# Direct maxima in the first five score units, and half of the score masks added by VectorE instead of by a product with the identity

## What is computed

```python
def _L0_xattn_ref(q, k, v, mask, Wq, bq, Wk, bk, Wv, bv, Wo, bo):
    query = _split_heads(q @ Wq.T + bq)
    key_ = _split_heads(k @ Wk.T + bk)
    value = _split_heads(v @ Wv.T + bv)
    scores = jnp.einsum('bhqd,bhkd->bhqk', query, key_) / jnp.sqrt(jnp.asarray(D_K, query.dtype))
    scores = jnp.where(mask == 0, jnp.asarray(NEG, scores.dtype), scores)
    attn = jax.nn.softmax(scores, axis=-1)
    ctx = jnp.einsum('bhqk,bhkd->bhqd', attn, value)
    return ctx.transpose(0, 2, 1, 3).reshape(...) @ Wo.T + bo

x = x + mixer(layernorm(x))
x = x + _L0_xattn_ref(layernorm(x), ctx_1024, ctx_1024, mask, ...)
x = x + experts(layernorm(x))
```

## Time and profile before

| What | Value |
|---|---|
| median of three runs | 418.87 us (418.56 to 420.62) |
| the profiled execution, its own time | 422.17 us |
| its span in the trace | 420.4 us |
| TensorE busy in the span | 356.0 us (85%) |
| VectorE busy | 262.3 us (62%) |
| ScalarE busy | 146.0 us (35%) |
| GpSimd busy | 144.6 us (34%) |
| mask products in the score stages (L1322) | 80 of 0.39 to 0.40 us each as modelled |
| fillers (L1296) | 64, 15.4 us busy |
| exponentials (L707) | 80, 0.600 us each |

### The profile page before, as it was taken

How to read it: one execution, slowest core, us unless ns; L and a number is a source line. 1 busy time by engine, 2 the same in 40 slices (tenths; PEclk the granted TensorE clock), 3 DMA queues, 4 the chain that set the end, 5 groups by cost and what they waited for, 6 DMA issues and landing times.

```text
span 420.4 us, 5562 instructions
## 1 busy us (share of the span) xinstructions
PE 356.0 (85%) x1896; PEld 235.4 (56%) x1909; DVE 262.3 (62%) x628; ACT 146.0 (35%) x276; POOL 144.6 (34%) x150
## 2 busy tenths in 40 slices
PE   1546678579987999779996899999999899999995
PEld 1333345343464535445454543687788688888883
DVE  6595376882297924971249831576779766666662
ACT  2503404816634265005531146222221323223221
POOL 7331213562012130011003020356354565666563
PEclk9985676979999999999798799999899999999998
DMA  4203650331004210153001200321100242220000
GB/s 109 68 1 81 174 192 1 94 72 38 2 0 115 54 37 0 40 122 93 0 2 50 94 16 2 125 51 50 50 27 25 68 123 69 82 64 26 27 0 25
DMA packets 22216, 23.84 MB, mean 57 GB/s; under 512 B 5117, under 2 KB 17341, under 8 KB 21973
## 3 DMA queue, kind: packets, MB, share of 16 engines
q1 hardware_dynamic: 21805, 23.29, 20.2%
q10 hardware_dynamic: 384, 0.20, 0.2%
HBM read 20.11 MB, written 3.18 MB: 55 GB/s over the span
## 4 chain that ended last, share of the span: by engine, by line
PE 60%; DVE 21%; ACT 5%; issue 4%; DMA 4%; POOL 4%; ACTq 1%; SPq 0%; POOLq 0%; DVEq 0%
DVE nmax_mask L984 6%; PE pC L1337 4%; PE pS L1322 4%; PE pC L1334 4%; PE pS L1319 3%; PE pS L268 3%; PE pS L270 3%; PE pS L269 3%; PE pG L1116 2%; PE pS L1286 2%; PE pA L268 2%; PE pS L1289 2%; PE pB L268 2%; PE pB L270 2%; PE pB L269 2%
## 5 line engine op out<-in xcount | busy, mean ns | idle before, releaser
L586 POOL TENSOR_TENSOR xi_lo<-xi_f,xi_hi 128x512 fp32r<-128x512 f32 x43 | 55.8, 1299 | 53.4 <-ACT xi_hi L739 53.2
L984 DVE TENSOR_REDUCE nmax_mask<-pS 128x3 f32<-128x462 f32 (+1 forms) x96 | 52.7, 578 | 18.1 <-PE pS L1289 17.2
L707 ACT ACTIVATE prob<-pS 128x512 f32<-128x512 f32 x80 | 42.4, 600 | 33.4 <-PE pS L1322 30.3
L739 ACT CAST xi_hi<-xi_f 128x512 fp32r<-128x512 f32 x43 | 26.7, 621 | 65.8 <-DVE xi_f L1039 65.8
L1039 DVE TENSOR_TENSOR xi_f<-sig,pS 128x512 f32<-128x512 f32 x64 | 44.0, 688 | 3.9 <-PE pS L270 0.6
L1286 PE MATMUL pS<-k_stack,q_stack 72*128 72x154 bf16 x256 | 36.7, 249 | 3.2 <-DMA q_stack<-q_scr 3.1
L586 POOL TENSOR_TENSOR act_lo<-xi_f,act_hi 128x512 fp32r<-128x512 f32 x21 | 27.5, 1310 | 27.1 <-ACT act_hi L739 27.1
L1289 PE MATMUL pS<-mbias,ident_bf 128*128 128x462 bf16 (+1 forms) x96 | 36.3, 378 | 0.0
L1286 PEld LDWEIGHTS pS<-k_stack,q_stack 72*128 72x128 bf16 x256 | 22.0, 107 | 12.1 <-issue 7.1
L1283 PE MATMUL pS<-mbiasT,ident_bf 128*128 128x128 bf16 x72 | 17.5, 243 | 11.7 <-DVE nmax_mask L984 11.4
L739 ACT CAST act_hi<-xi_f 128x512 fp32r<-128x512 f32 x21 | 13.0, 620 | 41.0 <-DVE xi_f L1039 41.0
(11 more groups left out here) (332 smaller groups left out, 846.3 us busy)
## 6 DMA issues: line engine op xcount, KB each, us to landing
prob<-w_scr SPq DMA_DIRECT2D x16, 256.0 KB, 3.3
q_stack<-q_scr SPq DMA_DIRECT2D x9, 384.0 KB
q_scr<-q_parts SPq DMA_DIRECT2D x12, 128.0 KB, 2.4
k_stack<-k_scr SPq DMA_DIRECT2D x36, 40.0 KB
res<-in_x_dram SPq DMA_DIRECT2D x4, 256.0 KB, 4.6
prob<-in_L_ffn_wg_dram SPq DMA_DIRECT2D x1, 1024.0 KB, 5.9
prob<-in_L_ffn_wp_dram SPq DMA_DIRECT2D x1, 1024.0 KB, 8.3
ctx_in<-in_L_ffn_wo_dram SPq DMA_DIRECT2D x4, 256.0 KB, 3.1
```

The source lines that it names most:

```text
L586: pool.tensor_tensor(hid_lo[u % NHID], hid[:, u % 2, :], f32(hid_hi[u % NHID]), ALU.subtract).then_inc(s_hidlo, 1)
L707: act.activation(prob[:, (NSB * b + n) % NBUF, :], score_bank(b, NSA + n)[:, :], ACT.Exp).then_inc(s_exp, 1)
L739: act.copy(hid_hi[u % NHID], hid[:, u % 2, :]).then_inc(s_hidhi, 1)
L984: dve.tensor_reduce(nmax[:, qt, hs[0]:hs[-1] + 1], score_bank(b, n)[:, 0:len(hs) * KEYS].rearrange("p (h k) -> p h k", k=KEYS), AX.X, ALU. ...
```

## The change

"keep_busy" is taken out. In its first place come the products over 72 rows and the masks of units 0 to 2 ("scores_early", EARLY = 3). The maxima of units 0 to 4 (DIRECT = 5) are not taken from rows of `q_stack` but added by one more product each, of `mT` (48 rows) with a 48 x 128 matrix of zeros and ones that sums the three parts of the right head: `head_rows` for a single head, `rest_rows` for the four. These wait for the copy to `mT` alone. Unit 5 waits for the rows of the DMA, which SP starts now instead of ScalarE, behind the query fetch of the same batch; in batch 3 the gate rows of experts 4 to 7 are moved behind them. Of the 20 units of a batch, units 3, 5, 6, 8, 10, 11, 13, 15, 16 and 18 have no mask product: VectorE adds the mask as it copies the bank to `prob`, and the exponential then reads and writes `prob`. ScalarE does that exponential one slot later than before, behind the exponential of the next unit where that one reads PSUM. `head_rows` and `rest_rows` are built by two reductions on VectorE ahead of batch 0's "max_split".

```diff
@@ -276,7 +279,29 @@
+        BY_PE, BY_DVE = range(2)
+        MASK_BY = [BY_PE] * 3 + [BY_DVE, BY_PE] + [BY_DVE, BY_DVE, BY_PE, BY_DVE, BY_PE] * (G - 1)
+        N_DVE = MASK_BY.count(BY_DVE)
...
+        DIRECT, EARLY = 5, 3
+        def exps_in(n):
+            late = [n - 1] if n > 0 and MASK_BY[n - 1] == BY_DVE else []
+            return ([] if MASK_BY[n] == BY_DVE else [n]) + late
+        EXP_ORDER = [u for n in range(NSB) for u in exps_in(n)]
+        assert sorted(EXP_ORDER) == list(range(NSB))
+        def exps_until(u):
+            return EXP_ORDER.index(u) + 1
+        def masked_until(u):
+            return MASK_BY[:u + 1].count(BY_DVE)
@@ -358,11 +383,10 @@
                 slots[u].append(("scores_max", b, u))
-            slots[NSA] += [("max_split", b, 0)]
+            slots[NSA] += [("max_split", b, 0)] + [("scores_early", b, u) for u in range(EARLY)]
...
-            slots[NSA] += [("keep_busy", b, 6)]
@@ -393,7 +417,6 @@
-            slots[B0 - 1] += [("keep_busy", b, 10)]
@@ -476,15 +499,28 @@
-                        for e in range(E):
-                            if e == 4:
-                                sp.wait_ge(s_pv, G * NB)
+                        for e in range(E // 2):
...
+                elif step == "max_rows":
+                    sp.wait_ge(s_mTc, b + 1)
+                    if b > 0:
+                        sp.wait_ge(s_mrow, 16 * PARTS * b)
+                    if b >= 2:
+                        sp.wait_ge(s_sb, NSB * (b - 1))
+                    for p_ in range(PARTS):
+                        sp.dma_start(q_stack[b % 2][MROW + p_:MROW + p_ + 1, :, :],
+                                     mT[p_ * H:(p_ + 1) * H, :]).then_inc(s_mrow, 16)
+                elif step == "weigh" and (b, n) == (NB - 1, G - 1):
+                    sp.wait_ge(s_pv, G * NB)
+                    for e in range(E // 2, E):
+                        fetch_gate(0, e)
@@ -692,20 +728,20 @@
-                    act.wait_ge(s_mTc, b + 1)
-                    for p_ in range(PARTS):
-                        act.dma_start(q_stack[b % 2][MROW + p_:MROW + p_ + 1, :, :],
-                                      mT[p_ * H:(p_ + 1) * H, :]).then_inc(s_mrow, 16)
                 elif step == "scores":
-                    act.wait_ge(s_sb, NSB * b + n + 1)
-                    before = NSB * b + n - NBUF
-                    if before >= 0:
-                        act.wait_ge(s_pv, before // 5 + 1)
-                    else:
-                        act.wait_ge(s_wsplit, EXPERT_STEPS)
-                    act.activation(prob[:, (NSB * b + n) % NBUF, :], score_bank(b, NSA + n)[:, :], ACT.Exp
-                                   ).then_inc(s_exp, 1)
+                    for u in exps_in(n):
+                        before = NSB * b + u - NBUF
+                        if MASK_BY[u] == BY_DVE:
+                            act.wait_ge(s_added, N_DVE * b + masked_until(u))
+                            src = prob[:, (NSB * b + u) % NBUF, :]
+                        else:
+                            act.wait_ge(s_sb, NSB * b + u + 1)
+                            if before >= 0:
+                                act.wait_ge(s_pv, before // 5 + 1)
+                            else:
+                                act.wait_ge(s_wsplit, EXPERT_STEPS)
+                            src = score_bank(b, NSA + u)[:, :]
+                        act.activation(prob[:, (NSB * b + u) % NBUF, :], src, ACT.Exp).then_inc(s_exp, 1)
@@ -833,6 +870,14 @@
             for step, b, n in STEPS:
+                if step == "max_split" and b == 0:
+                    dve.wait_ge(s_ident, 1)
+                    dve.tensor_reduce(head_rows[:, :],
+                                      ident[0:PARTS * H, 0:PARTS * H].rearrange("p (a h) -> p h a", a=PARTS),
+                                      AX.X, ALU.max)
+                    firsts = ident[0:PARTS * H, 0:PARTS * H].rearrange("p (a h) -> p h a", a=PARTS)[:, 0:4, :]
+                    dve.tensor_reduce(rest_rows[:, :].rearrange("p (c k) -> p c k", c=4)[:, :, 0:K1],
+                                      firsts.unsqueeze(2).broadcast_to([PARTS * H, 4, K1, PARTS]), AX.X, ALU.max)
@@ -998,6 +1043,16 @@
+                elif step == "scores" and MASK_BY[n] == BY_DVE:
+                    u = NSB * b + n
+                    dve.wait_ge(s_sb, u + 1)
+                    if u >= NBUF:
+                        dve.wait_ge(s_pv, (u - NBUF) // 5 + 1)
+                    else:
+                        dve.wait_ge(s_wsplit, EXPERT_STEPS)
+                    bias = mbiasT_rem if SB_UNITS[n][1] is None else mbiasT
+                    dve.tensor_tensor(prob[:, u % NBUF, :], score_bank(b, NSA + n)[:, :], bias[:, :], ALU.add
+                                      ).then_inc(s_added, 1)
@@ -1124,7 +1179,41 @@
                     else:
-                        pe.wait_ge(s_exp, NSB * row + k - NSA + 1)
+                        u = k - NSA
+                        if MASK_BY[u] == BY_DVE:
+                            pe.wait_ge(s_added, N_DVE * row + masked_until(u))
+                        else:
+                            pe.wait_ge(s_exp, NSB * row + exps_until(u))
+            def score_products(b, n, rows):
+                g, j = SB_UNITS[n]
+                whole = rows == DEEP
+                by_pe = MASK_BY[n] == BY_PE
+                bank_free(b, NSA + n)
+                dst = score_bank(b, NSA + n)
+                if j is None:
+                    for c in range(4):
+                        last = pe.matmul(dst[Q * c:Q * (c + 1), :], k_stack[b % 2][0:rows, 4 * g + c, K0:KPAD],
+                                         q_stack[b % 2][0:rows, 4 * g + c, :], start=True, stop=whole and not by_pe,
+                                         skip_group_check=True)
+                    bias = mbiasT_rem
+                else:
+                    last = pe.matmul(dst[:, :], k_stack[b % 2][0:rows, 4 * g + j, 0:K0],
+                                     q_stack[b % 2][0:rows, 4 * g + j, :], start=True, stop=whole and not by_pe,
+                                     skip_group_check=True)
+                    bias = mbiasT
+                if by_pe:
+                    last = pe.matmul(dst[:, :], ident_bf[:, :], bias[:, :], start=False, stop=whole,
+                                     skip_group_check=True)
+                return last
+            def less_max(b, n):
+                g, j = SB_UNITS[n]
+                assert g == 0
+                rows = rest_rows[:, :] if j is None else head_rows[:, j:j + 1].broadcast_to([PARTS * H, P])
+                return pe.matmul(score_bank(b, NSA + n)[:, :], rows, mT[:, :],
+                                 start=False, stop=True, skip_group_check=True)
@@ -1303,24 +1392,20 @@
+                elif step == "scores_early":
+                    score_products(b, n, STACK)
...
-                    g, j = SB_UNITS[n]
                     if n == 0:
+                        pe.wait_ge(s_mTc, b + 1)
+                    elif n == DIRECT:
...
-                    bank_free(b, NSA + n)
-                    dst = score_bank(b, NSA + n)
-                    if j is None:
-                        for c in range(4):
-                            pe.matmul(dst[Q * c:Q * (c + 1), :], k_stack[b % 2][:, 4 * g + c, K0:KPAD],
-                                      q_stack[b % 2][0:DEEP, 4 * g + c, :], start=True, stop=False, skip_group_check=True)
-                        bias = mbiasT_rem
-                    else:
-                        pe.matmul(dst[:, :], k_stack[b % 2][:, 4 * g + j, 0:K0], q_stack[b % 2][0:DEEP, 4 * g + j, :],
-                                  start=True, stop=False, skip_group_check=True)
-                        bias = mbiasT
-                    pe.matmul(dst[:, :], ident_bf[:, :], bias[:, :], start=False, stop=True, skip_group_check=True
-                              ).then_inc(s_sb, 1)
+                    if n >= EARLY:
+                        last = score_products(b, n, STACK if n < DIRECT else DEEP)
+                    if n < DIRECT:
+                        last = less_max(b, n)
+                    last.then_inc(s_sb, 1)
```

4 lines of the change are left out of this document (added).

## The result

The changed kernel takes **425.57 us** (median of 4 runs, 422.37 to 427.08) against 419.06 us (4 runs, 418.56 to 420.62) for the kernel before: a ratio of **1.0131**, 95% interval 1.0096 to 1.0167. The forecast was 415.2 us with a range up to 420.8. The change makes the kernel 1.3% slower. The profiled execution took 422.37 us, the shortest of the four, with a mean granted clock of 0.901; the others had 0.897, 0.889 and 0.889. The profiled execution of before (422.17 us, clock 0.926) was longer than every timed one of that kernel. So the two profiles nearly agree in length (420.6 and 420.4 us of span), and their difference must not be read as the change's.

The account below looks back on a forecast made before the run. TensorE was taken as never free in the score stages, ScalarE as second limit, VectorE late at batches 1 to 3. Batches of -2.5, +2.6, -4.0, +0.2 gave -3.7: profiled 422.17 to 418.5, hence 415.2 us, range 411.2 to 420.8.

Parts of the forecast that it names:

- The clock: TensorE's clock at batch starts without fillers: one fall, in batch 1 after a 4.1 us gap, +1.7 us; none elsewhere.
- Rival (b): Clock falls in batches 2 and 3 also, 1.5 us each, and reductions miss their slot: 418.2 to 419.5 us; chance 0.28.
- Rival (c): TensorE, idle 0.8 us in each group, loses its clock inside the groups: +7.8, 423 us; chance 0.12.
- Unit 3's mask add: VectorE's add behind xn_post sets weigh 0 through an exponential: +1.0, -2.7, -0.4 us in batches 1 to 3.
- Groups: Weigh to weigh, ScalarE's copy and four exponentials set the period: 4.86 against 4.79 us, +0.14 a batch.
- last group of batch 3: End of batch 3's score stage: the last weigh follows the fourth exponential instead of the third, +0.5 us.
- exit of a stage: End of the score stages of batches 0 to 2: unit 18's mask saved ahead of the next maxima, -0.2 us.
- rival (d): In the groups masks count in full, ScalarE's order being no limit: about 7.5 us further down, 407.7 us; chance 0.08.
- Batch 0: Start of batch 0's score stage: weigh 0 at 97.09 against 99.54 us, -2.4.
- The expert stage: Experts after the last weigh: unchanged and moving along, so no term in the sum.
- The reference level: Profile of before stood 3.3 us above its median; the same difference takes the forecast from 418.5 to 415.2 us.
- Setup, queues: Two reductions ahead of batch 0's max_split cost 0 (1.3 if late); moved DMA issues cost 0 (2 us if late).

Follow-up runs that it names:

- again: The changed kernel run and profiled once more, unedited: 424.76 us, ratio 1.0119 to the kernel before.
- masks_only: The kernel before, fillers kept and no direct maxima, with only VectorE's ten masks a batch put in: 422.10 us, ratio 1.0047.
- before_norm_early: The kernel before with only VectorE's norm moved ahead of values, mixer's sum and statistics in batches 1 and 2: 419.47 us, ratio 1.0003.
- unit3_pe: The changed kernel with unit 3 masked by TensorE's product again, nine masks a batch left on VectorE: 419.30 us, ratio 0.9956.
- direct_only: The changed kernel with every mask added by TensorE's product again; direct maxima stay, fillers stay out: 418.09 us, ratio 0.9957.
- after_warm: The changed kernel with ten thrown-away filler products ahead of unit 6's product in batches 1 to 3: 420.84 us, ratio 1.0020.
- unit3_only: The changed kernel with only unit 3's mask on VectorE, the other nineteen on TensorE: 428.40 us, ratio 1.0221.
- late_masks: The changed kernel with VectorE masking only units 10, 11, 13, 15, 16, 18, its norm earlier, exponentials 11 and 16 ahead of the copy: 408.66 us.
- no_fillers: The kernel before with only the filler products taken out: 423.02 us, ratio 1.0062.
- late_plain: The changed kernel with VectorE masking only units 10, 11, 13, 15, 16 and 18, both orders left as changed: 418.78 us, ratio 0.9956.
- unit3_warm: The changed kernel with unit 3 masked by TensorE and eight filler products behind unit 6's product in batches 1 to 3: 418.74 us, ratio 0.9980.

## Why the prediction was wrong, step by step

Each batch from the transposes of its maxima to its last weigh, in us against the kernel before:

| | forecast | profile after | again |
|---|---|---|---|
| batch 0 | -2.5 | -1.2 | -0.9 |
| batch 1 | +2.6 | +3.5 | +2.4 |
| batch 2 | -4.0 | -3.0 | -2.2 |
| batch 3 | +0.2 | +1.7 | +2.7 |
| sum | -3.7 | +1.1 | +2.0 |

**The clock (the step that failed most).** The text counted one fall, in batch 1, and said of the others "in batch 2 the gap is about what it is now, in batch 3 unit 5 breaks it; none counted". The fall in batch 1 came as forecast, and 1.7 us was about its size (weigh 0 to weigh 1 longer by 2.1 and 1.0 us). But the clock fell in batch 3 too (0.62 at 244 to 248 us, behind a gap of 2.20 us: unit 5 did not break it, since unit 6 waited), which made weigh 0 to weigh 1 longer by 1.2 and 1.9 us. It fell in batch 2 as well (0.50 at 192 to 196): weigh 0 to weigh 2, which was to be some 1.1 us shorter, was 0.9 us shorter in one profile and 0.4 us longer in the other. The evidence I had, a gap of 2.6 us that was followed by no fall, was one case, in a stretch ahead of which fillers had run, as they had ahead of gaps of 1.50 us (masks_only, batch 1) and 2.17 us (before_norm_early, batch 2) that no fall followed; unit3_pe fell behind 2.38 us and direct_only behind 1.95. after_warm shows the size of the whole: 1.0%. Rival (b), with 0.28, had the right half of the mechanism, the falls in batches 2 and 3; its other half did not happen (the reductions ended at 81.63 us, ahead of GpSimd's instruction at 81.98), and its 418.2 to 419.5 us is still 6 us short. Rival (c) had the nearest number, 423 us, and not the mechanism: inside the groups, at 99.00 to 112.70 us, the clock stayed at 1.00 with TensorE busy 12.89 of 13.70 us. The page cited from the Trainium skill ("TensorE: Matmul & The Clock Gate", Part 1), by which activity releases the clock, was the better guide: after_warm agrees with it, 1.00 where it was 0.50, by products that compute nothing.

**Unit 3's mask add.** The sizes were nearly right: +1.0 for batch 1, measured +1.35; -2.7 for batch 2, measured -2.1 and -2.6; -0.4 for batch 3, measured -0.25 and 0.0. The chain was not: "before weigh 0 of batches 1 to 3 the wait should be for an exponential". Exponential 3 ended earlier than the weigh; it was unit 6's product, which needs unit 3's bank, and the transposes behind it that came last, at half clock. I had looked at who needs the result of the add and not at who needs its bank. That is what makes TensorE idle, and so one mask in ten carries the loss (unit3_pe, unit3_only).

**Groups.** Forecast 4.86 us, measured 4.87 and 4.88, with the wait for the exponential; last group of batch 3 +0.65 where +0.5 was forecast; exit of a stage, -0.12 where -0.2 was forecast. This step held, and so did the answer to rival (d). late_masks shows how much of (d) can be had once ScalarE's order and VectorE's place are mended: all of the two products ahead of weigh 1 (0.44 us), and 0.38 of 0.65 us in the group behind it.

**Batch 0.** Weigh 0 gained 1.2 and 0.9 us instead of 2.4. In these profiles the stretch ahead of it ran at 0.50 (84 to 88 us), in that of before at 0.82; that the fixed prices, taken at full clock, were too low there fits these rows, and no run tests it.

**The expert stage, put at nothing.** "The expert stage after the last weigh is unchanged and moves along" failed: it took 1.59 us longer at the same mean clock of 0.98, and 3.00 us longer in "again", where one more stretch was at low clock. The first part is no scatter. In the last half of the stage, from ScalarE's 37th last cast to its last one, the 17 traces of kernels built from the changed one all show 76.22 to 76.24 us, and the three built from the kernel before (its own, no_fillers, before_norm_early) 75.43 to 75.45. Before, and then after:

```profile
337.53:412.96 75.43, 75.43 (x334) 61.57 (x332) 51.06 (x74) 23.31 (x38) 46.89 (x36) 1.00 0.17 50
```

```profile
337.09:413.32 76.23, 76.23 (x334) 61.64 (x333) 51.02 (x74) 23.29 (x38) 46.79 (x36) 1.00 0.16 47
```

These are the same 334 products at a clock of 1.00. The difference is there with no mask on VectorE (direct_only) and with the fillers kept (masks_only), so neither brings it. What these 17 have in common, among other things, is the two new tiles with their reductions, the new semaphore and the later fetch of gate rows; no run took these apart, and the cause is open.

**The reference level.** "[S]o the same difference gives 415.2 us" took the level of one profile as given. Outside the score stages and the experts the traces scatter: the maxima of batch 0 are transposed at 87.60 us in the profile of before, at 85.5 to 87.0 in all others, and from batch 2's last weigh to batch 3's maxima it is 23.65 us there, 21.63 and 21.03 in the two of the changed kernel. One part of it is not chance: the stretch from batch 0's last weigh to batch 1's maxima took 23.9 us in all four traces of kernels with the fillers of the kernel before, and 24.4 to 26.3 in all but one (unit3_pe) of those without. There the clock was down to between 0.5 and 0.9 somewhere from 120 to 136 us. The forecast had no term for a stage that the change does not touch. Added up, the profile after is +1.1 us in the score stages, +1.6 in the experts and -2.5 in the rest, "again" +2.0, +3.0 and -2.9. Of the 10.4 us between forecast and result, 4.8 to 5.7 thus lie in the score stages and 1.6 to 3.0 in the experts. The 3.3 us that were taken off for the profile of before lie in runs of which there is no trace.

**Setup, queues.** Nothing in the traces speaks against 0 for either as far as weigh 0 goes: the rows of the maxima held unit 5 up by 1.54 us in batch 2 (190.62 us), but unit 6 waited for VectorE after that. That wait is part of the idle time ahead of the low clock in batch 2, though.

What stays open: what slows the expert stage, why the medians of late_plain and unit3_warm did not follow their shorter stages, and why removing fillers at the border of batch 0 is followed by low clock 35 us later. No run told these apart. unit3_warm also limits what is said of the clock: with unit 3 back on TensorE the fillers mended the row (6.95 to 4.77 us in batch 1) and not the time.

## What to carry to other kernels

When work goes to another engine, ask who waits for the buffer it frees, not only for its result: with three banks one mask add behind 2.8 us of other work stopped TensorE 3.5 us, and cost more than nine others gained (1.0221 with that one alone, 0.9957 with none, 1.0119 and 1.0131 with all ten). Place such work only where that engine has nothing in front of it, and set the consumers' order anew; here direct maxima with six masks in the late groups and two orders mended gave -2.4%, ten masks spread over all groups +1.3%. Products that compute nothing may be holding the clock; before they go, the gap that remains has to go too, and every stage start should be priced with the fall and without. And a stage that no line of the edit names is to be compared too: here the experts gave 1.6 us of the loss.

## What the hardware showed that I had not expected

TensorE's granted clock fell to 0.50 behind gaps of 1.95, 2.2, 2.4 and 3.5 us at the starts of score stages, and what followed ran for 3 to 6 us at twice its duration (1.91 us for a pair of 1.02), so that weigh 0 to weigh 1 alone was longer by 1 to 2 us each time. Ten extra products in the gap, which take 2.33 us, kept it at 1.00 though TensorE stood idle 1.26 us more; a gap of 1.10 us (unit3_pe, batch 3) was followed by no fall either. The same program's runs differ by up to 6 us (direct_only: 414.35 to 420.45) and go with their mean clock, though loosely: its three at 0.927 took 414.4 to 414.7, its two at 0.904 took 418.1 and 420.5, but one at 0.916 took 419.8.
